# A mixture of experts followed by a gated recurrence: column tiles of 32 for all matmuls, narrower recurrent products, and a later start of the expert work

## What is computed

```
shared = silu(x @ w1) * (x @ w3) @ w2                  # hidden size 512
s      = sigmoid([x, cond] @ router_W)                 # 8 experts, the best 2 by s + bias
routed = sum_e combine[:, e] * gelu(x @ W1e[e]) @ W2e[e]  # hidden size 256
x1     = x + (shared + routed) / 3

Z  = sigmoid(xz_t + H @ Whz.T + bhz)                   # 512 steps, one after another
R  = sigmoid(xr_t + H @ Whr.T + bhr)
Ht = tanh(xh_t + (R * H) @ Whh.T + bhh)
H  = Z * H + (1 - Z) * Ht                              # H is 8 x 256, H0 = cond
out_t = x1_t + H @ Whq.T + bhq
```

## Time and profile before

| | |
|---|---|
| median of 3 runs | 1475.49 us |
| lowest, highest | 1471.8, 1476.03 us |
| the profiled execution | 1468.71 us |
| its span, first to last instruction | 1466.8 us |
| mean granted TensorE clock | 0.995 |
| TensorE matmul busy | 1423.3 us (97%) |
| VectorE, ScalarE busy | 1096.2 us (75%), 807.5 us (55%) |

### The profile page before, as it was taken

One profiled execution on the slowest core, in us unless ns is written; L12 is line 12 of the kernel. 1 busy time (PEld: TensorE's weight loads), 2 busy tenths in 40 slices (PEclk: granted clock), 3 DMA queues, 4 the chain that ended last, 5 costly groups with the idle time before them and its releaser, 6 DMA issues.

```text
span 1466.8 us, 73746 instructions
## 1 busy us (share of the span) xinstructions
PE 1423.3 (97%) x30336; PEld 1083.4 (74%) x30336; DVE 1096.2 (75%) x6673; ACT 807.5 (55%) x4317; POOL 6.7 (0%) x26
## 2 busy tenths in 40 slices
PE   1799999999999999999999999999999999999998
PEld 1697777777777777777777777777777777777765
DVE  0577777777777777777777777777777777777765
ACT  1445555655555565555555555555555555555543
POOL 0100000000000000000000000000000000000000
PEclk9999999999999999999999999999999999999999
DMA  9711111111111111111111111111111111111110
GB/s 132 228 45 28 34 39 43 27 43 43 32 35 38 43 37 32 43 38 34 35 41 38 31 43 39 35 34 39 41 29 43 43 32 34 40 41 29 35 32 13
DMA packets 66559, 63.87 MB, mean 44 GB/s; under 512 B 14001, under 2 KB 61617, under 8 KB 66225
## 3 DMA queue, kind: packets, MB, share of 16 engines
q1 hardware_dynamic: 66224, 59.17, 16.4%
HBM read 25.46 MB, written 16.78 MB: 29 GB/s over the span
## 4 chain that ended last, share of the span: by engine, by line
PE 95%; DMA 2%; SPq 2%; DVE 1%; issue 0%; ACT 0%; DVEq 0%
PE bank L915 31%; PE bank L836 29%; PE bank L867 18%; PE bank L894 8%; PE bank L923 3%; PE bank L908 3%; DMA x_all<-in_x 1%; SPq L329 1%; PE bank L884 1%; DMA xT_cur<-xT_all 1%; PE bank L771 1%; DMA gates_cur<-gates_all 0%; SPq L356 0%; PE bank L788 0%; DVE acc L652 0%
## 5 line engine op out<-in xcount | busy, mean ns | idle before, releaser
L836 PE MATMUL bank<-xT_cur,we_sb 128*128 128x128 f32 x2048 | 345.6, 292 | 2.5 <-DVE hid L632 2.5
L478 ACT ACTIVATE t_r<-bank 128x32 f32<-128x32 f32 x1024 | 146.3, 195 | 359.4 <-PE bank L915 359.4
L696 DVE STREAM_TRANSPOSE t_rT<-t_r 128x32 f32<-128x32 f32 x1024 | 156.1, 191 | 225.9 <-ACT t_r L478 225.9
L915 PE MATMUL bank<-whT,hist 128*8 128x64 f32 x16384 | 324.8, 220 | 0.0
L836 PEld LDWEIGHTS bank<-xT_cur,we_sb 128*128 128x128 f32 x2048 | 268.6, 191 | 39.9 <-DVE hid L632 2.7
L915 PEld LDWEIGHTS bank<-whT,hist 128*8 128x8 f32 x16384 | 231.8, 89 | 83.4 <-DVE hist L724 30.2
L463 ACT ACTIVATE bank<-gru_raw 128x64 f32<-128x64 f32 (+1 forms) x1024 | 258.1, 252 | 19.8
L497 ACT ACTIVATE t_h<-bank 128x32 f32<-128x32 f32 x1024 | 146.5, 195 | 195.8 <-PE bank L915 184.6
L915 PEld LDWEIGHTS bank<-whT,rhT 128*8 128x8 f32 x8192 | 117.1, 88 | 134.7 <-DVE rhT L699 111.0
L915 PE MATMUL bank<-whT,rhT 128*8 128x64 f32 x8192 | 210.0, 220 | 1.3 <-DVE rhT L699 1.3
L721 DVE STREAM_TRANSPOSE terms<-t_h 128x32 f32<-128x32 f32 x1024 | 156.4, 191 | 55.4 <-ACT t_h L497 16.8
(11 more groups left out here) (99 smaller groups left out, 1418.6 us busy)
## 6 DMA issues: line engine op xcount, KB each, us to landing
gate_inputs_by_token<-gru_raw SPq DMA_DIRECT2D x32, 384.0 KB, 2.5
gru_raw<-gate_inputs_by_token SPq DMA_DIRECT2D x256, 48.0 KB
x_all<-in_x SPq DMA_DIRECT2D x16, 256.0 KB, 15.7
xT_cur<-xT_all SPq DMA_DIRECT2D x32, 128.0 KB, 2.0
x_cur<-x_all SPq DMA_DIRECT2D x32, 128.0 KB, 2.0
x_all<-x_cur SPq DMA_DIRECT2D x32, 128.0 KB, 2.3
gru_raw<-x_all SPq DMA_DIRECT2D x32, 128.0 KB, 2.2
out<-gru_raw SPq DMA_DIRECT2D x32, 128.0 KB
```

The costliest lines, as they stand in the source:

```text
L478: act.activation(t_r[:, i, :], r_ps[:, i * Q:(i + 1) * Q], ACT.Tanh, scale=0.5).then_inc(tr_ready, 1)
L696: dve.transpose(t_rT[:, i, :], t_r[:, i, :]).then_inc(trT_done, 1)
L836: last = pe.matmul(up_ps[place % ring][:, half * P:(half + 1) * P], w, xT_cur[:, k, :], start=(k == 0), stop=(k == KC - 1))
L915: last = pe.matmul(ps[Q * j:Q * j + B, col:col + GW], lhsT[:, i, :], whT[:, gate, i, j * GW:(j + 1) * GW], start=False, stop=(i == NI - 1) ...
```

## The change

- All matmuls that worked on the full array (`up`, `down`, the transposition of x1, `project`, `output`, `keep_busy`) go through `product`: four calls with 32 weight columns each, one per column tile, and 128 columns moved. One such group of four is a part.
- The down products of the experts are plain fp32, four parts an expert; the split into high and low, the second GELU and the low-part subtraction are gone.
- `chain_ps` has three banks: half 0 of r and c, half 1 of r and c, and z. r and c are computed half by half of their output (32 columns moved), and each half has its own signal, so the order of the columns in `wxT`, the biases and `xs` is changed to match. One seed (`seed_rc`) fills r and c after t_h, another (`seed_z`) z.
- (1 - z) factors: ScalarE makes `a_row` from t_z, VectorE transposes it straight into `factors`.
- `up` has two banks. The order of all fill is one list, SHARES, dealt out 3 parts to gap 1 and 3 or 4 to gap 2. A tile's work begins at gap 2 of step 6 (before: step 0) and runs over the end of the iteration; `kind'` in the list is work of the tile before.
- x_all, xT_all and gates_all are read in place and x1 is accumulated in x_all, without copies. `xs`, `xproj`, `yst` and others no longer lie over the raw weights.

The diff, cut to its core:

```diff
-        r_ps, zc_ps = bank[0], bank[1]
-        up_ps = bank[2:5]
-        dn_ps = bank[5:7]
-        misc = bank[7]
+        chain_ps = ctx.enter_context(nc.psum_tensor("chain_ps", [P, 3, 512], F32))
+        up_ps = [ctx.enter_context(nc.psum_tensor(f"up_ps{i}", [P, 512], F32)) for i in range(2)]
+        dn_ps = [ctx.enter_context(nc.psum_tensor(f"dn_ps{i}", [P, 512], F32)) for i in range(2)]
+        misc = ctx.enter_context(nc.psum_tensor("misc", [P, 512], F32))
...
+        SHARES = [("up", 0, 4), ("down'", 7, 4), ("down'", 8, 4), ("up", 1, 4), ("x1'", 0, 2), ("up", 2, 4),
+                  ("proj'", 0, 4), ("proj'", 1, 4), ("proj'", 2, 4), ("up", 3, 4), ("up", 4, 4), ("out", 0, 4),
+                  ("up", 5, 4), ("down", 0, 8), ("up", 6, 4), ("down", 1, 4), ("up", 7, 4), ("down", 2, 4),
+                  ("up", 8, 4), ("down", 3, 4), ("up", 9, 4), ("down", 4, 4), ("up", 10, 4), ("down", 5, 4),
+                  ("up", 11, 4), ("down", 6, 4)]
+        COUNT1 = [3] * TS
+        COUNT2 = [4, 3, 4, 3, 4, 3, 4, 4, 4, 4, 4, 4, 4, 3, 3, 3]
+        FIRST_STEP, FIRST_PARTS = 6, 2
...
+        UP_ACT1 = {1: 7, 6: 11, 7: 0, 12: 3}
+        UP_ACT2 = {2: 8, 3: 9, 4: 10, 8: 1, 9: 2, 12: 4, 13: 5, 15: 6}
+        SILU1 = {9: 1, 10: 2}
+        SILU2 = {7: 0, 12: 3}
+        HIDDEN2 = {7: 0, 9: 1, 10: 2, 12: 3}
+        ADD1 = {3: 3, 4: 4, 8: 7, 15: 0}
+        ADD2 = {0: 1, 1: 2, 5: 5, 6: 6, 8: 8}
+        BIAS1 = {11: 1}
+        BIAS2 = {10: 0, 11: 2}
...
-                        act.wait_ge(r_done, TS * n + s + 1)
                         for i in range(NI):
-                            act.activation(t_r[:, i, :], r_ps[:, i * Q:(i + 1) * Q], ACT.Tanh, scale=0.5).then_inc(tr_ready, 1)
+                            act.wait_ge(r_done, NI * (TS * n + s) + i + 1)
+                            act.activation(t_r[:, i, :], chain_ps[:, i, 0:Q], ACT.Tanh, scale=0.5).then_inc(tr_ready, 1)
...
+                        act.wait_ge(tz_ready, TS * n + s + 1)
+                        act.activation(a_row[:, :, :], t_z[:, :, :], ACT.Copy, bias=0.5, scale=-0.5).then_inc(a_ready, 1)
...
+                        seed_z(*after)
+                    if outs and s == 0:
+                        keep_states(n - 1)
...
+                        for i in range(NI):
+                            act.wait_ge(c_done, NI * (TS * n + s) + i + 1)
+                            act.activation(t_h[:, i, :], chain_ps[:, i, Q:2 * Q], ACT.Tanh, scale=-1.0).then_inc(th_ready, 1)
                     if after:
-                        seed_zc(*after)
+                        seed_rc(*after)
...
-                        dve.wait_ge(tz_ready, TS * n + s + 1)
-                        dve.transpose(t_zT[:, :, :].rearrange("p i q -> p (i q)"), t_z[:, :, :].rearrange("p i q -> p (i q)"))\
-                           .then_inc(tzT_done, 1)
+                        dve.wait_ge(a_ready, TS * n + s + 1)
+                        dve.transpose(factors[:, :, :, 1].rearrange("p i q -> p (i q)"), a_row[:, :, :].rearrange("p i q -> p (i q)"))\
+                           .then_inc(aT_done, 1)
...
+                    if s in ADD1 and 0 <= added_tile(n, s, ADD1[s]) < NT:
+                        accumulate(added_tile(n, s, ADD1[s]), ADD1[s])
+                    if proj and s in BIAS1:
+                        add_bias(n + 1, BIAS1[s])
+                    if outs and s == Y_STEP:
+                        finish_out(n - 1)
                     if scan:
-                        dve.wait_ge(tzT_done, TS * n + s + 1)
-                        dve.tensor_scalar(factors[:, :, :, 1], t_zT[:, :, 0:B], -0.5, 0.5, ALU.mult, ALU.add).then_inc(a_ready, 1)
...
+            def product(ps, col, lhsT, rhs, first, last):
+
+                for j in reversed(range(NG)):
+                    done = pe.matmul(ps[Q * j:Q * (j + 1), col:col + P], lhsT[:, Q * j:Q * (j + 1)], rhs,
+                                     start=first, stop=last, tile_position=(0, Q * j), skip_group_check=True)
+                return done
...
+            def gate_product(i, k, h, col, gate, lhsT, cols):
 
                 for j in reversed(range(NG)):
-                    last = pe.matmul(ps[Q * j:Q * j + B, col:col + GW], lhsT[:, i, :],
-                                     whT[:, gate, i, j * GW:(j + 1) * GW], start=False, stop=(i == NI - 1),
+                    done = pe.matmul(chain_ps[Q * j:Q * j + B, i, col:col + cols], lhsT[:, k, :],
+                                     whT[:, gate, k, j * GW + h:j * GW + h + cols], start=False, stop=(k == NI - 1),
                                      tile_position=(0, Q * j), skip_group_check=True)
...
+                        pe.wait_ge(seeded_rc, TS * n + s + 1)
                         for i in range(NI):
+                            for k in range(NI):
+                                if i == 0:
+                                    pe.wait_ge(hT_ready, g + k + 1)
+                                done = gate_product(i, k, Q * i, 0, 0, hT, Q)
+                            done.then_inc(r_done, 1)
+                        pe.wait_ge(seeded_z, TS * n + s + 1)
+                        for k in range(NI):
+                            done = gate_product(NI, k, 0, 0, 1, hT, GW)
+                        done.then_inc(z_done, 1)
+                    fill(n, GAP1[s], scan)
                     if scan:
                         for i in range(NI):
-                            pe.wait_ge(rhT_ready, g + i + 1)
-                            if i == 0:
-                                pe.wait_ge(tz_ready, TS * n + s + 1)
-                            last = gate_product(zc_ps, GW, 2, rhT, i)
-                        last.then_inc(c_done, 1)
+                            for k in range(NI):
+                                if i == 0:
+                                    pe.wait_ge(rhT_ready, g + k + 1)
+                                done = gate_product(i, k, Q * i, Q, 2, rhT, Q)
+                            done.then_inc(c_done, 1)
+                    fill(n, GAP2[s], scan)
```

More of the change, by code:

```diff
@@ L152, in moe_then_gru @@
         ld_we1 = sem("ld_we1")
-        ld_we2 = [sem(f"ld_we2_{part}") for part in range(3)]
+        ld_we2 = sem("ld_we2")
         ident0 = sem("ident0")
@@ L472, in body, with copy_x1T @@
+            def copy_x1T(t):
+                act.wait_ge(x1T_done, t + 1)
+                act.activation(x1T[:, :, :].rearrange("p k t -> p (k t)"), misc[:, 0:C], ACT.Copy).then_inc(x1T_ready, 1)
+            def body(n, scan, proj, outs):
                 for s in range(TS):
-                    after = (n, s + 1) if s + 1 < TS and scan else (n + 1, 0) if s + 1 == TS and proj else None
+                    m = tile_of(n, s)
+                    last = s + 1 == TS
+                    after = (n, s + 1) if scan and not last else (n + 1, 0) if proj and last else None
@@ L494, in body @@
-                    if scan:
-                        act.wait_ge(c_done, TS * n + s + 1)
-                        for i in range(NI):
-                            act.activation(t_h[:, i, :], zc_ps[:, GW + i * Q:GW + (i + 1) * Q], ACT.Tanh, scale=-1.0).then_inc(th_ready, 1)
-                    if scan and s == HALF - 2:
-                        act.wait_ge(xs_second, 16 * NG * (n + 1))
-                    if proj and s == TS - 2:
-                        act.wait_ge(xs_first, 16 * NG * (n + 2))
@@ L900, in output @@
[L900 to L912 removed]
+                done = product(up_ps[place % 2], half * P, w, xT_all[:, m, k, :], k == 0, k == KC - 1)
@@ new lines, in fill @@
+            def fill(n, gap, scan):
+                for p in gap:
+                    m = n + 2 if p >= 0 else n + 1
+                    kind, i, part = PARTS[p]
+                    if kind == "up" and 0 <= m < NT:
+                        up(m, i, part)
+                    elif kind == "down" and 0 <= m < NT:
+                        down(m, i, part)
+                    elif kind == "down'" and 1 <= m <= NT:
+                        down(m - 1, i, part)
+                    elif kind == "x1'" and 1 <= m <= NT:
+                        transpose_x1(m - 1, part)
+                    elif kind == "proj'" and 1 <= m <= NT:
+                        project(m - 1, i, part)
+                    elif kind == "out" and 3 <= m <= NT + 2:
+                        output(m - 3, part)
+                    elif scan and m >= NT:
+                        keep_busy()
@@ L917, in gate_product, with keep_busy @@
                                      tile_position=(0, Q * j), skip_group_check=True)
-                return last
-            def keep_busy(count):
-                for _ in range(count):
-                    pe.matmul(up_ps[0][:, 0:2 * P], zeros[:, :], w1_sb[:, 0, 0:2 * P], start=True, stop=True).then_inc(kept_busy, 1)
-            def body(n, scan, moe, proj, outs, more):
+                return done
+            def keep_busy():
+                pe.wait_ge(gelu_ready, NE * NT - 1)
```

(1 more changed line is left out.)

570 lines of the change are left out of this document (218 added, 352 removed).

## The result

The changed kernel takes **2177.81 us** (median of 4 runs, 2174.44 to 2183.76), the kernel before 1475.76 (4 runs): a ratio of 1.477, 95% interval 1.4729 to 1.4812. The forecast was 1288 us in a range from 1240 to 1430. It was wrong in sign, and by 890 us.

What follows compares the result with a forecast made beforehand. TensorE, busy 97%, was taken to bound the kernel through its 2.656 us step; 88 before the first step + 512 x 2.315 + 5.7 after gave a 1279 us span, 1288 us as median, range 1240 to 1430.

Steps and rivals of the forecast that it cites:

- rival D: TensorE's instruction supply: records rise from 118 to 266 a step, a 16 KB block needed every 2.2 us; slower, chance 0.03.
- Narrow passes: Halved r and c products: a 32-column pass taken as 0.030 us, making r 0.24, z 0.22, c 0.24.
- rival B: Halves of r and c buy nothing, a 32-column pass costing the 0.056 of 64 columns: near 1430 us, chance 0.12.
- Tiled parts: Fill as 32-column tiles running side by side: 0.111 us a pass of 128 columns, 0.222 a part.
- The switches go: TensorE's changes between column tiles and full array, 0.30 us a pair, two pairs a step, vanish: -0.60 a step.
- rival C: Switches stay, the array draining between 8-column gate tiles and 32-column fill tiles: 2.77 us a step, 1521 us, chance 0.05.
- ACT and DVE hand-overs (E): z, a_row and fill consumers queue in the first gap, losing 0.15 us more a step: about 1360 us, chance 0.14.
- the seed of r and c: After both t_h: starts 0.22 us after the second, takes 0.28, ready about 0.04 before the state.
- A: The forecast itself, 1288 us, chance 0.60; its best, 0.028 a narrow pass and no extras, gives 1245 us.
- six wide instructions: 256-wide VectorE instructions in six of 16 steps' first gaps delay factors: +0.12 less 0.04 each, 0.56 us in all.
- The first gap's switches: One of the two switch pairs a step, before c, credited with 0.30 us of the 0.60 saved.
- Signs named ahead: Right: r products 2.2 to 2.35 us apart, TensorE above 95% busy; wrong: among others, semaphore-free holes inside groups.

Runs made afterwards that it cites:

- e11: e7 with up calls moved from the second gap to the first and F32R down products moved to the second: 1408.22 us, ratio 0.9565 to the kernel before.
- e5: Kernel before plus 16 tiny calls a step (64 records, 8 weight and 8 moved columns) ahead of z: 1644.51 us, ratio 1.1151.
- e7: Kernel before with the first gap's fp32 calls as four column tiles, F32R calls and second gap unchanged: 1470.66 us, ratio 0.9992.
- e3: Changed kernel with all fill back on the full array and r and c not halved: 1542.75 us.
- e4: Changed kernel with r and c not halved, fill tiled in the first gap only, full array in the second: 1508.69 us, ratio 1.0236 to the kernel before.

## Why the prediction was wrong

**The step that failed** is rival D's: "240 blocks of 16 KB, 1.17 us each ... A block would be needed every 2.2 us; that fits unless a block is only asked for when the last is used up." The need was right (256 records in 2.1 us). The block's price was not: I took the duration of its transfer, and what decides is the round trip, request, transfer and hand-over, 1.21 + 1.13 + 1.38 us with only one block under way. The kernel before gave no row for that, since its blocks were used in 5.57 us; it bounded the price from above, by 5.6 (by 4.12, had I taken its two blocks nearest to each other), and I should have carried both ends, 1.17 and 5.6 us, into the range. With the upper one a step of 266 records is 5.8 us. The condition "asked for only when the last is used up" got 0.03 and no time; with the number now measured it is 266 x 15.2 ns = 4.04 us a step, 512 x 4.04 = 2068, with 88 to 103 ahead and 6 behind about 2170. Measured: first r at 102.97, last at 2167.22, 4.04 a step.

Why a transfer is only asked for about 1.2 us into the block before it isn't visible in any row; that no more than one is ahead is read from the times alone. The Trainium skill (Runtime: NRT & Kernel Launch, Instruction fetch mechanics) says that the sequencer fetches the next 16 KiB block while it executes the current one and that crossing into it is mostly hidden. Size and look-ahead agree with the traces here (16 KB, 256 records); "hidden" holds at 5.6 us a block (before) and at 4.8 (e11), and not where TensorE uses a block up in less than 3.8.

**The other terms held, beneath the supply.** They are read in stretches without a hole.
- *Narrow passes:* 0.029 us (forecast 0.030; rival B's 0.056 is out). r to t_r takes 0.38 (0.37), c to t_h 0.42 (0.37). Below 32 columns the cost stops following them: passes of four tiles with 8 moved columns in e5 lie 0.026 us apart, and the eight of them moved z's start by 0.034 each. The Trainium skill's rule in columns (TensorEngine Tiling (Array Packing), Instruction Overhead) isn't borne out between 32 and 64 columns; a floor of that kind shows between 8 and 32.
- *Tiled parts:* 0.109 us a 128-column pass (0.111).
- *The switches go:* the first fill matmul starts 5 ns after z's last one; rival C is out for these tile shapes. In the kernel before the first full call starts 0.149 after the last gate record, where in e7 a tiled call starts 0.035 after it, so the way in costs 0.11, with 0.10 more in the first full pass, and the way back 0.09: the 0.30 a pair of the sum.
- *ACT and DVE hand-overs (E):* not tested at the forecast's speed, since the shortest step of after is 3.14 us. But its legs can be read in stretches without a hole over 0.25 us (medians): r to t_r 0.38, t_r to c 0.74, c to t_h 0.42, t_h to the next r 0.82. That is 2.35 us, where the sum had 2.21 for this path and 2.26 for the step. Most of it is one term, put at nothing: the seed of r and c starts 0.23 after the second t_h and takes 0.28, as forecast, but r starts 0.15 after the seed's end and not at once. So t_h to r is 0.82 instead of 0.71; in e11, which seeds r early, it goes down to 0.72. By this the step would have been about 2.35 without the supply (an estimate from those legs; with the first r at 88 to 103 it makes some 1310 to 1320 us), between A and E.
- *Slips of the sum, all small:* six wide instructions at 0.12 less 0.04 are 0.48 and not 0.56 us per tile (2.6 us in the total); A's best comes to 1249 by its own terms, not 1245; C and D together are 0.08 where "slower" has 0.07. The first r was forecast at 88 and came at 102.97; even e3, with neither tiles nor halves, has it at 95.91.
- *The first gap's switches*, half of the 0.60 a step that I credited: e7 shows that in the kernel before they were worth nothing by themselves: TensorE was through this gap about when rhT came, and the 111 us that the weight loads waited for rhT were not free time of the array (the page of before has 1.3 us of idle time of the matmuls there). The gain could only come from moving work across, which the new order did.
- *Signs named ahead:* "holes inside groups with no semaphore (D)" is exactly what came; a busy share above 95% and 2.2 to 2.35 us a step did not.

So a forecast of the array's own time was right to a few per cent, and the time was set by something of which the kernel before used 70% (3.85 of 5.57 us a block).

## What to carry to other kernels

Before matmuls are split into column tiles or narrower pieces, count records (matmuls and weight loads, twice each in fp32) per step: here TensorE got a block of 256 every 3.8 to 3.9 us on the mean at best, about 15 ns a record, so a 2.6 us step had room for some 170, not 266, and with 158 to 160 (e4) uneven steps still ran into it. Tile only where the engine switches and where there is slack in that budget, and take the widest moved operand that the work allows. Time saved in a gap that ends in a wait is worth nothing until work is moved into it (0.999, then 0.957 with the counts).

## What the runs showed that was not expected

- Instruction supply binds TensorE: 3.79 us from block to block (median), 853 us of holes in 2177, the transfers never two at a time. In bursts TensorE took records at 8 ns (256 in 2.1 us).
- Calls with 8 weight columns and 8 moved columns are no free filler: 32 fp32 calls added to each step of before cost 1.18 us a step (1472.6 to 2075.4 us over 512 steps), 16 cost 0.34.
- No drain shows between tiles with 8 weight columns and tiles with 32 at the same column positions (5 ns).
- The granted clock of after averages 0.978 (before 0.995 over its whole span), with 19 stretches of 3.4 to 6.8 us at half the clock (1.2 GHz) between its first and last r, 75 us in all, where before has none; that is small beside the holes.
